# A five-block transformer stack on one core: the last feed-forward block works on one tile of tokens behind the other, and three row maxima of the attention passes stand in other units

## The chip, the core and the metric

The program runs on one core of one Trainium2 chip. The core has five engines with a queue of instructions each: TensorE (PE, matmuls; PEld is its weight load), VectorE (DVE), ScalarE (ACT), GpSimd (POOL) and SyncE (SP), which here issues every DMA. They meet only at semaphores. The metric is the device time of one execution in microseconds (us), lower is better.

## The reference, cut to what matters

One sequence of 256 tokens with 512 features, and a context of 4096 rows of 128 features, pass six residual blocks. The change touches the fourth in part, the fifth's last steps and the whole of the sixth:

```python
x = x + _L0_xattn_ref(_layernorm(x), ctx_512, ...)
x = x + _L0_attn_ref(_layernorm(x), ...)
x = x + _L0_ffn_ref(_layernorm(x), ...)      # 32 experts
x = x + _L1_xattn_ref(_layernorm(x), ctx_512, ...)   # 16 heads over 4096 keys
x = x + _L1_attn_ref(_layernorm(x), ...)     # gated state space; its output is y * rsqrt(mean(y*y)+eps) @ W_out
x = x + _L1_ffn_ref(_layernorm(x), w_gate_up, w_down)

def _quant_dequant(v, axis):                 # 8 bits, one scale for each row
    scale = jnp.max(jnp.abs(v), axis=axis, keepdims=True) / 127.0
    scale = jnp.maximum(scale, 1e-8)
    return jnp.clip(jnp.round(v / scale), -127, 127) * scale
def _L1_ffn_ref(x, w_gate_up, w_down):       # 512 -> 2 * 1408 -> 512
    gate_up = quant(x) @ quant(w_gate_up).T
    gate, up = split(gate_up)
    h = silu(gate) * up
    return quant(h) @ quant(w_down).T
```

The scale of a token's inner row `h` needs the maximum over all 1408 inner values before any of them can be rounded.

## The kernel before, in words

Each engine's program is written out by hand, block after block; nothing is scheduled by a planner. A wait on a semaphore holds up all that stands behind it on its engine.

**The fourth block** (attention over 4096 keys) runs in `XP = 8` passes over pairs of heads, each of `NCH = 8` units `c` of 512 keys, each unit of four quarters `e`. In a quarter PE turns a tile of probabilities (`turn`), ACT takes it out of PSUM (`pH`, line 856), DVE takes the low part (`pL`, line 1198), and PE weighs the values with both (`weigh`). Beside that, pass `p` makes the scores of pass `p + 1`, which DVE copies out with their maxima (`scores_out`, line 1145): four tiles in each of the units 1 to 7 (those of the unit ahead), none in unit 0, and in unit 7 the four of the last unit as well, followed by the row maxima `nmX` without which ACT cannot start the exponentials. Units 3 to 6 also add a finished output to `x` on DVE (`add_out`, line 1157).

In the same passes the weights of the sixth block are quantized in the background: 15 jobs (`JOBS`), three in a pass, so passes 0 to 4. `row_max` on DVE takes the maximum of 128 rows in two halves (line 1164, in quarters 1 and 3 of the unit), and the scale and its inverse (lines 1170, 1172); SP stores them and loads the next rows (`rows`); POOL rounds a tile of the weights (`round_columns`) and SP stores it (`columns`). `ROWS_AT` names the three units: 1, 4 and 7. The halves are of 704 elements in the first four jobs (pass 0 and the first job of pass 1) and of 512 in the others.

**The fifth block's end.** For eight tiles `m` DVE makes `yz`, ACT `yn` and its square `y2`; POOL sums the squares, and PE multiplies `yn` with `wout` (`project`, line 1753). PE sums the squares over partitions (lines 1778, 1779), DVE and POOL make the root `yrs`, and DVE adds the projected rows, times `yrs`, to `x` (line 1296).

**The sixth block** has two tiles `t` of 128 tokens. LayerNorm of both, one `row_scales` over both (lines 1221 to 1223), rounding in fp32 by adding and subtracting a constant (`xr` on DVE, `xq` on ACT), eight transposes on PE, one copy `xqT` on ACT. Then eight chunks `n`, four for each token tile, of 352 gate and 352 up columns: eight matmuls (line 1799), `gs` and `us` on DVE, Silu on ACT (`sgF`), the product `hF` on POOL. After a token tile's four chunks: the maximum over 1408 elements on DVE (`hs`), rounding (`hr`, `hq`), eleven transposes (line 1806), the copy `hqT` on ACT, eleven matmuls with `w_down` (line 1812), `of` and `x` on DVE. `swb` holds the weights' scales, broadcast to all partitions. One DMA stores `out`. `stay_awake(count, bank)` (line 1339) issues `count` matmuls of 512 columns on constants whose result nobody reads; they stand where PE would wait.

Of the kernel before, what the change touches and what calls it, by code (L numbers as in the profile page):

```python
# [92 lines left out]
def perceiver(nc, a, out):  # L93
    ctx = ExitStack()
    with ctx:
# [578 lines left out]
        def _(act):  # L674
# [273 lines left out]
            act.wait_ge(late_pe.sem, late_pe.at("xqT", 1))
            act.activation(xqT[:], PSb[:, 0, :].rearrange("p (k t) -> p k t", t=T), ACT.Copy).then_inc(late_act.sem, 1)

            def integers(t):
                act.wait_ge(hr_ready, t + 1)
                act.activation(hq[:, t], hr[:, t], ACT.Copy, bias=-ROUND).then_inc(hq_ready, 1)
# [8 lines left out]
            for t in range(NT):  # L962
                if t:
                    integers(t)
                act.wait_ge(late_pe.sem, late_pe.at("hqT", t + 1))
# [935 lines left out]
```

## Time and profile before

| | |
|---|---|
| median of 3 runs | 1056.04 us (1053.2 to 1057.41) |
| profiled execution, its own time | 1053.18 us |
| its span | 1051.5 us |
| busy: PE, DVE, ACT, POOL | 94%, 70%, 55%, 28% of the span |
| chain that ended last | PE 76%, DVE 14%, ACT 5%, issue 2% |
| fourth block's passes | 440 to 935 us of the span |
| fifth block | 936 to 1013 us |
| sixth block | 1013 to 1051.5 us |

Busy times are shares of the span; the chain of waits is followed back from the last instruction, and only what lies on it can shorten the kernel. The program's own time is 1.7 us above the span.

### The profile page before, as it was taken

How to read it: one execution, taken by the hardware profiler on the slowest of the kernel's cores; microseconds unless marked ns; L12 is line 12 of the kernel's file. 1: busy time of each engine (PE TensorE's matmuls, PEld its weight loads, DVE VectorE, ACT ScalarE, POOL GpSimd, SP SyncE). 2: the span in 40 equal slices, each digit the busy share in tenths (PEclk: the TensorE clock that was granted, in tenths of full speed). 3: DMA queues.
4: the chain of work that ended last, by engine and by line, in shares of the span. 5: the costliest groups of instructions: out<-in, count | busy, mean ns of one | idle time of the engine just before them, and what ended most of it. 6: DMA issues, size and time to landing. Idle time of an engine off the chain costs nothing.

```text
span 1051.5 us, 18010 instructions
## 1 busy us (share of the span) xinstructions
PE 990.6 (94%) x6641; PEld 788.4 (75%) x6641; DVE 732.6 (70%) x1434; ACT 575.1 (55%) x1251; POOL 291.2 (28%) x210
## 2 busy tenths in 40 slices
PE   7989989999998799999998999989899999989996
PEld 5545689999997576687787777878788787968653
DVE  3566456555553789788787888878877787658555
ACT  3445344444443320486776667767676777837633
POOL 6910144444442300000000422313225504013412
PEclk9999999999999999999999999999999999999999
DMA  8560076656632233201113347423323203083010
GB/s 269 130 242 1 4 231 245 213 210 209 209 121 82 83 95 101 71 29 28 52 46 54 61 92 103 91 53 77 76 58 95 72 1 96 8 295 162 1 66 21
DMA packets 65966, 109.18 MB, mean 104 GB/s; under 512 B 19393, under 2 KB 44129, under 8 KB 64738
## 3 DMA queue, kind: packets, MB, share of 16 engines
q1 hardware_dynamic: 65890, 108.17, 35.3%
q8 instruction: 47, 0.77, 0.3%
q14 instruction: 29, 0.24, 0.1%
HBM read 103.24 MB, written 4.91 MB: 103 GB/s over the span
## 4 chain that ended last, share of the span: by engine, by line
PE 76%; DVE 14%; ACT 5%; issue 2%; DMA 1%; POOL 1%; SPq 0%; DVEq 0%; ACTq 0%; POOLq 0%
PE PS L1618 14%; PE PS L1491 12%; PE PS L1607 9%; PE PS L1595 8%; PE PS L1510 5%; DVE scores L1145 3%; PE PS L1580 3%; PE PS L1710 3%; PE PS L1632 2%; PE PS L1339 2%; DVE pL L1198 2%; PE PS L1753 1%; ACT scores L832 1%; PE PS L1391 1%; PE PS L1550 1%
## 5 line engine op out<-in xcount | busy, mean ns | idle before, releaser
L1198 DVE TENSOR_TENSOR pL<-PS,pH 128x512 fp32r<-128x512 f32 x256 | 175.9, 687 | 66.0 <-ACT pH L856 65.5
L856 ACT ACTIVATE pH<-PS 128x512 fp32r<-128x512 f32 x256 | 151.7, 595 | 99.9 <-PE PS L1607 99.9
L832 ACT ACTIVATE scores<-scores,nmX 128x512 f32<-128x512 f32 x256 | 185.2, 723 | 26.3 <-DVE nmX L1149 26.3
L1145 DVE TENSOR_SCALAR_CACHE_REDUCE scores<-PS 128x512 f32<-128x512 f32 x256 | 172.6, 682 | 18.8 <-PE PS L1595 18.4
L1618 PE MATMUL PS<-pH,kvH 128*128 128x256 f32 x512 | 164.4, 321 | 7.4 <-ACT xnT L841 7.4
L1607 PE MATMUL PS<-ident,scores 128*128 128x128 f32 x1024 | 157.3, 276 | 4.5 <-DVE pL L1198 4.3
L1607 PEld LDWEIGHTS PS<-ident,scores 128*128 128x128 f32 x1024 | 117.0, 140 | 36.6 <-issue 16.4
L1618 PE MATMUL PS<-pL,kvH 128*128 128x256 f32 x512 | 143.9, 281 | 0.0
L1618 PE MATMUL PS<-pH,kvL 128*128 128x256 f32 x512 | 143.7, 281 | 0.0
L1618 PEld LDWEIGHTS PS<-pH,kvH 128*128 128x128 f32 x512 | 96.7, 189 | 11.6 <-issue 11.4
L614 POOL TENSOR_TENSOR xn<-xn,winvB 128x1024 f32<-128x1024 f32 (+1 forms) x17 | 39.6, 2330 | 211.0 <-DMA xn<-in_w1t 114.3
L1618 PEld LDWEIGHTS PS<-pL,kvH 128*128 128x128 f32 x512 | 97.2, 190 | 0.0
L1618 PEld LDWEIGHTS PS<-pH,kvL 128*128 128x128 f32 x512 | 96.4, 188 | 0.0
L1052 DVE TENSOR_TENSOR gL<-rawG,gH 128x1536 fp32r<-128x1536 f32 x16 | 56.9, 3554 | 29.4 <-ACT gH L715 29.3
L578 POOL TENSOR_TENSOR dL<-rawD,dH 128x1536 fp32r<-128x1536 f32 x16 | 56.4, 3526 | 47.1 <-ACT dH L759 47.1
L1595 PE MATMUL PS<-keyH,qsH 64*128 64x512 f32 x256 | 58.4, 453 | 8.6 <-DVE scores L1145 8.2
L1491 PE MATMUL PS<-xH,gH 128*128 128x256 f32 x192 | 54.7, 285 | 3.2 <-DVE uL L1052 2.9
L599 POOL TENSOR_TENSOR wkrL<-wkr,wkrH 128x128 fp32r<-128x128 f32 x8 | 4.2, 524 | 191.0 <-ACT wkrH L796 191.0
L1595 PEld LDWEIGHTS PS<-keyH,qsH 64*128 64x128 f32 x256 | 24.0, 183 | 42.9 <-issue 24.5
L1491 PE MATMUL PS<-xH,uH 128*128 128x256 f32 x192 | 54.9, 286 | 0.0
L1491 PE MATMUL PS<-xL,uH 128*128 128x256 f32 x192 | 54.9, 286 | 0.0
L1491 PE MATMUL PS<-xH,uL 128*128 128x256 f32 x192 | 54.9, 286 | 0.0
(305 smaller groups left out, 2250.1 us busy)
## 6 DMA issues: line engine op xcount, KB each, us to landing
rawG<-in_wg SPq DMA_DIRECT2D x16, 768.0 KB, 5.7
rawU<-in_wu SPq DMA_DIRECT2D x16, 768.0 KB, 7.2
rawD<-in_wd SPq DMA_DIRECT2D x16, 768.0 KB, 6.4
wrow<-in_w SPq DMA_DIRECT2D x11, 512.0 KB, 5.5
xn<-in_w1t SPq DMA_DIRECT2D x11, 512.0 KB
wturned<-turned SPq DMA_DIRECT2D x4, 1056.0 KB, 13.5
wb<-w_rows SPq DMA_DIRECT2D x32, 128.0 KB, 3.3
wqX<-in_wqX SPq DMA_DIRECT2D x16, 256.0 KB, 2.6
```

Of the source, the lines that this page charges most:

```text
L578: pool.tensor_tensor(dL[:, b].rearrange("p m n -> p (m n)"), rawD[:, b], dH[:, b].rearrange("p m n -> p (m n)").bitcast(F32), ALU.subtract ...
L614: step(pool.tensor_tensor(part.rearrange("p (k o) -> p k o", o=shape[2]), part.rearrange("p (k o) -> p k o", o=shape[2]), inverse, ALU.mult))
L832: act.activation(at, at, ACT.Exp, bias=nmX[:, p % 2, h, q:q + 1], accum_out=csum[:, p % 2, NT * h + q, c:c + 1]).then_inc(exp_done, 1)
L856: act.activation(pH[:, i % 4], PS[:, 2 + i % 2, :].rearrange("p (k t) -> p k t", t=T), ACT.Copy).then_inc(pH_ready, 1)
L1052: dve.tensor_tensor(lo[b][:].rearrange("p k m n -> p (k m n)"), raw[:, b], hi[b][:].rearrange("p k m n -> p (k m n)").bitcast(F32), ALU.su ...
L1145: dve.tensor_scalar(sp_[:, h, q, c * CH:(c + 1) * CH], PS[:, 4 * q + h, :], 1.0, None, ALU.mult, ALU.max, accum_out=cmax[:, h, q, c:c + 1] ...
L1198: dve.tensor_tensor(pL[:, i % 4], PS[:, 2 + i % 2, :].rearrange("p (k t) -> p k t", t=T), pH[:, i % 4].bitcast(F32), ALU.subtract).then_in ...
L1491: mm = pe.matmul(PS[:, 3 * b + m, j * T:(j + 1) * T], w[b][:, kt, m, :], v[:, kt, :], start=(kt == 0 and c == 0), stop=(kt == KT - 1 and c ...
L1510: mm = pe.matmul(PS[:, 6 + t, :], h[:, b, m, t * P:(t + 1) * P], w[:, b, m, :], start=(first and m == 0 and c == 0), stop=(last and m == 2 ...
L1595: mm = pe.matmul(PS[:, 4 * q + h, :], w[rank, p % 2, q * P:(q + 1) * P], v[rank, c * CH:(c + 1) * CH], start=(j == 0), stop=(j == 2), skip ...
L1607: mm = pe.transpose(PS[:, 2 + i % 2, m * T + q * P:m * T + (q + 1) * P], sp_[:, h, q, tile * P:(tile + 1) * P], ident[:])
L1618: mm = pe.matmul(PS[:, 6, h * T:(h + 1) * T], w[:, 4 * c + 2 * u + m, :], v[:, i % 4, m, :], start=(i == 0 and m == 0 and k == 0), stop=(c ...
```

## The change

`ROWS_AT` becomes 1, 3, 5. In the sixth block the two token tiles run one behind the other: tile 0's input is normalized, rounded, turned and copied alone, and tile 1's follows in ACT's and PE's queues behind the first two chunks. The maximum over 1408 is taken in four of 352 (`chunk_max`), each two chunks late, and then over those four. Rounding, transposes, copies and the second product are cut into parts (`PARTS`): two for tile 0, three for tile 1, one of whose copies is DVE's. `stay_awake` goes from 6 to 0 ahead of the last projection, from 40 to 24 and from 4 to 3 about the input's transposes, from 8 to 0 ahead of tile 0's inner transposes, and from 8 to 10 ahead of tile 1's. The sums of squares move ahead of the last projection. `swb` is laid over the dead weights `win` and loaded as soon as these are read; the output is stored tile by tile.

```diff
-ROWS_AT = (1, 4, 7)
+PARTS = (((0, 8, 6), (8, FT, 7)), ((0, 4, 4), (4, 8, 5), (8, FT, 2)))
+ROWS_AT = (1, 3, 5)
...
-        swb = A("swb", [P, (GT + DT) * P])
+        swb = win[:].rearrange("p k n -> p (k n)")[:, 0:(GT + DT) * P]
+        hmx = A("hmx", [P, NT, 4])
...
-            sp.wait_ge(x_done, 5)
-            sp.dma_start(swb[:], s_rows[:].partition_broadcast(P)).then_inc(swb_in, 16)
-            sp.wait_ge(x_done, 6)
-            sp.dma_start(out.rearrange("o (t p) d -> p (o t) d", p=P), x[:]).then_inc(stored, 16)
-            sp.wait_ge(stored, 16)
+            sp.wait_ge(ssm_pe.sem, ssm_pe.at("z3", 1))
+            sp.dma_start(swb, s_rows[:].partition_broadcast(P)).then_inc(ffn_in, 16)
+            for t in range(NT):
+                sp.wait_ge(x_done, 6 + t)
+                sp.dma_start(out.rearrange("o (t p) d -> p (o t) d", p=P)[:, t], x[:, t]).then_inc(stored, 16)
+            sp.wait_ge(stored, 16 * NT)
...
+            input_integers(0)
             for n in range(4 * NT):
                 act.wait_ge(gs_ready, n + 1)
                 if n >= 2:
                     act.wait_ge(hF_ready, n - 1)
                 act.activation(sgF[:, n % 2], gs[:, n % 2], ACT.Silu, scale=sx[:, n // 4:n // 4 + 1]).then_inc(late_act.sem, 1)
+                if n == 1:
+                    input_integers(1)
                 if n == 6:
-                    integers(0)
...
+                    integers(0, 0)
+                    integers(0, 1)
+            turned_part(0, 0)
+            turned_part(0, 1)
+            integers(1, 0)
+            integers(1, 1)
+            turned_part(1, 0)
+            integers(1, 2)
+            turned_part(1, 2)
...
+            gated_out(0)
+            ln_stats(0)
+            gated_out(1)
             dve.sem_inc(x_done, 1)
...
+            input_rounded(0)
+            ln_stats(1)
+            input_rounded(1)
+            dve.wait_ge(ffn_in, 80)
+
+            def chunk_max(n):
+                t, c = n // 4, n % 4
+                dve.wait_ge(hF_ready, n + 1)
+                dve.tensor_reduce(hmx[:, t, c:c + 1], hF[:, t, c * FC:(c + 1) * FC], AX.X, ALU.max, apply_absolute_value=True).then_inc(dve_step, 1)
+                step.n += 1
 
             def rounded(t):
-                dve.wait_ge(hF_ready, 4 * (t + 1))
-                row_scales(hs[:, t:t + 1], hsi[:, t:t + 1], hF[:, t])
-                dve.tensor_scalar(hr[:, t], hF[:, t], hsi[:, t:t + 1], ROUND, ALU.mult, ALU.add).then_inc(hr_ready, 1)
+                dve.wait_ge(dve_step, step.base + step.n)
+                row_scales(hs[:, t:t + 1], hsi[:, t:t + 1], hmx[:, t])
+                for a_, b_, bank in PARTS[t]:
+                    dve.tensor_scalar(hr[:, t, a_ * P:b_ * P], hF[:, t, a_ * P:b_ * P], hsi[:, t:t + 1], ROUND, ALU.mult, ALU.add).then_inc(hr_ready, 1)
...
+                if n >= 2:
+                    chunk_max(n - 2)
                 if n == 5:
                     rounded(0)
+            chunk_max(4 * NT - 2)
+            chunk_max(4 * NT - 1)
             rounded(1)
+            a_, b_, bank = PARTS[1][1]
+            dve.wait_ge(late_pe.sem, late_pe.at("hqT1", 2))
+            dve.tensor_copy(hqT[:, a_:b_, P:T], PSb[:, bank, 0:(b_ - a_) * P].rearrange("p (k t) -> p k t", t=P)).then_inc(hqT_mid, 1)
...
+            stay_awake(24, 4)
+            pe.wait_ge(late_dve.sem, late_dve.at("ms", 1))
+            turn_input(0)
+            stay_awake(3, 4)
+            pe.wait_ge(late_act.sem, late_act.at("xqT0", 1))
+            pe.wait_ge(ffn_in, 80)
             for n in range(4 * NT):
                 t, c = n // 4, n % 4
                 if n >= 2:
                     pe.wait_ge(us_ready, n - 1)
+                if n == 2:
+                    turn_input(1)
+                if n == 4:
+                    pe.wait_ge(late_act.sem, late_act.at("xqT1", 1))
...
+            turn_part(0, 0)
+            turn_part(0, 1)
+            pe.wait_ge(hqT_ready, 1)
+            down_part(0, 0)
+            pe.wait_ge(hqT_ready, 2)
+            down_part(0, 1)
             pe.wait_ge(us_ready, 4 * NT)
-            stay_awake(8, 2)
-            turn_inner(1)
-            down_inner(1)
+            stay_awake(10, 2)
+            turn_part(1, 0)
+            turn_part(1, 1)
...
```

**DVE in pass 4, unit 7.** `pL` is the low part of the probabilities, `scores,cmax` a tile of the next pass's scores with its maximum, `nmX` the row maximum, `wmax`, `wscale`, `winv` the weight rows' job. Before:

```order
L1164 TENSOR_REDUCE wmax<-wrow 128x1 [waits wrow_in]
L1145 TENSOR_SCALAR scores,cmax<-PS 128x512 [waits sX_ps]
L1139 TENSOR_TENSOR keyL<-PS,keyH 128x512 [waits keyH_ready]
L1198 TENSOR_TENSOR pL<-PS,pH 128x512 [waits pH_ready]
L1145 TENSOR_SCALAR scores,cmax<-PS 128x512 [waits sX_ps] x2
L1149 TENSOR_REDUCE nmX<-cmax 128x1 [waits sX_out]
L1145 TENSOR_SCALAR scores,cmax<-PS 128x512 [waits sX_ps]
L1149 TENSOR_REDUCE nmX<-cmax 128x1 [waits sX_out]
L1198 TENSOR_TENSOR pL<-PS,pH 128x512 [waits pH_ready]
L1164 TENSOR_REDUCE wmax<-wrow 128x1
L1170 TENSOR_SCALAR wscale<-wmax 128x2 [waits scale_stored,dve_step]
L1172 RECIPROCAL winv<-wscale 128x2 [waits wscale_ready]
```

Now, the same stretch:

```order
L1158 TENSOR_TENSOR keyL<-PS,keyH 128x512 [waits keyH_ready]
L1217 TENSOR_TENSOR pL<-PS,pH 128x512 [waits pH_ready]
L1164 TENSOR_SCALAR scores,cmax<-PS 128x512 [waits sX_ps] x2
L1168 TENSOR_REDUCE nmX<-cmax 128x1 [waits sX_out]
L1164 TENSOR_SCALAR scores,cmax<-PS 128x512 [waits sX_ps]
L1168 TENSOR_REDUCE nmX<-cmax 128x1 [waits sX_out]
L1217 TENSOR_TENSOR pL<-PS,pH 128x512 [waits pH_ready]
L1164 TENSOR_SCALAR scores,cmax<-PS 128x512 [waits sX_ps]
L1168 TENSOR_REDUCE nmX<-cmax 128x1 [waits sX_out]
```

The two reductions and the two small operations behind them are gone from here.

**DVE in pass 4, unit 5**, the unit to which they move (now; `x<-PS,recX,x` is the addition of a finished output):

```order
L1183 TENSOR_REDUCE wmax<-wrow 128x1 [waits wrow_in]
L1164 TENSOR_SCALAR scores,cmax<-PS 128x512 [waits sX_ps]
L1158 TENSOR_TENSOR keyL<-PS,keyH 128x512 [waits keyH_ready]
L1217 TENSOR_TENSOR pL<-PS,pH 128x512 [waits pH_ready]
L1164 TENSOR_SCALAR scores,cmax<-PS 128x512 [waits sX_ps]
L1217 TENSOR_TENSOR pL<-PS,pH 128x512 [waits pH_ready]
L1183 TENSOR_REDUCE wmax<-wrow 128x1
L1189 TENSOR_SCALAR wscale<-wmax 128x2 [waits scale_stored,dve_step]
L1191 RECIPROCAL winv<-wscale 128x2 [waits wscale_ready]
```

They stand between the same neighbours as they do in unit 4 of before.

**PE at the end of the fifth block and the start of the sixth.** `busyB` rows are those of `stay_awake`, `ones` rows the sums of squares, `wout,yn` the last projection, `identb,xq` the input's transposes. Before:

```order
L1753 MATMUL PS<-wout,yn 128x512 [waits yn_ready]
L1753 MATMUL PS<-wout,yn 128x512
L1339 MATMUL PS<-busyB,identE 128x512 x6
L1753 MATMUL PS<-wout,yn 128x512 [waits yn_ready]
L1778 MATMUL PS<-ones,y2s 128x1 [waits decay_ready,y2_ready,y2_added]
L1779 MATMUL PS<-ones,y 128x1
L1778 MATMUL PS<-ones,y2s 128x1
L1779 MATMUL PS<-ones,y 128x1
L1753 MATMUL PS<-wout,yn 128x512
L1339 MATMUL PS<-busyB,identE 128x512 x40
```

Now:

```order
L1793 MATMUL PS<-wout,yn 128x512 [waits yn_ready]
L1793 MATMUL PS<-wout,yn 128x512
L1815 MATMUL PS<-ones,y2s 128x1 [waits decay_ready,y2_ready,y2_added]
L1816 MATMUL PS<-ones,y 128x1
L1815 MATMUL PS<-ones,y2s 128x1
L1816 MATMUL PS<-ones,y 128x1
L1793 MATMUL PS<-wout,yn 128x512 [waits yn_ready]
L1793 MATMUL PS<-wout,yn 128x512
L1379 MATMUL PS<-busyB,identE 128x512 x24
L1826 MATMUL PS<-identb,xq 128x128 [waits late_act,late_dve]
L1826 MATMUL PS<-identb,xq 128x128 x3
L1379 MATMUL PS<-busyB,identE 128x512 x3
```

The sums of squares now stand ahead of both projections, and the first token tile is turned alone; the second tile's four transposes stand behind sixteen matmuls of the first two chunks.

## Rows read from the trace of the kernel before

**Rows 1.** The page: span and instructions.

```profile
span 1051.5 us, 18010 instructions
```

**Rows 2.** Timeline, ACT: `pH` opening unit 7 and the next pass; start, length.

```profile
490.08 0.60 ACT L856 ACTIVATE pH<-PS 128x512 fp32r<-128x512 f32 x1 [1.49 <-PE PS L1607]
501.31 0.58 ACT L856 ACTIVATE pH<-PS 128x512 fp32r<-128x512 f32 x1
...
748.71 0.60 ACT L856 ACTIVATE pH<-PS 128x512 fp32r<-128x512 f32 x1 [1.49 <-PE PS L1607]
759.35 0.58 ACT L856 ACTIVATE pH<-PS 128x512 fp32r<-128x512 f32 x1
...
813.21 0.60 ACT L856 ACTIVATE pH<-PS 128x512 fp32r<-128x512 f32 x1 [1.49 <-PE PS L1607]
822.40 0.58 ACT L856 ACTIVATE pH<-PS 128x512 fp32r<-128x512 f32 x1
```

**Rows 3.** Chain that ended last, pass 4 unit 7: start, length, what.

```profile
751.24 0.59 DVE wmax L1164
```

**Rows 4.** Windows: units 4, 4, 5, 6 of passes 4, 5, 4, 4; busy by engine.

```profile
726.00:733.90 7.90, 7.90 (x60) 6.42 (x59) 7.30 (x19) 5.47 (x14) 3.94 (x3) 1.00 0.01 2
790.50:798.40 7.90, 7.90 (x60) 6.42 (x59) 6.38 (x15) 5.47 (x14) 3.94 (x3) 1.00 0.31 60
733.90:741.80 7.90, 7.90 (x59) 6.42 (x59) 6.78 (x15) 5.47 (x14) 0.00 (x0) 1.00 0.81 137
...
741.80:748.80 7.00, 7.00 (x57) 6.15 (x57) 5.70 (x13) 5.44 (x14) 3.19 (x2) 1.00 0.55 147
```

**Rows 5.** Timeline, all engines, end of fifth block and input of sixth.

```profile
1007.06 0.40 ACT L938 ACTIVATE y<-yz 128x256 f32<-128x256 f32 x1
...
1010.38 0.16 DVE L1291 TENSOR_SCALAR ss<-PS 128x2 f32<-128x2 f32 x1 [3.78 <-PE PS L1779]
...
1011.15 8.80 PE L1339 MATMUL PS<-busyB,identE 128*128 128x512 bf16 x40
...
1011.43 1.54 DVE L1296 SCALAR_TENSOR_TENSOR x<-PS,yrs,x 128x512 f32<-128x512 f32 x2 [0.88 <-POOL yrs L666]
...
1018.34 0.88 DVE L1304 TENSOR_SCALAR xr<-xn,sxi 128x512 f32<-128x512 f32 x2
1018.86 1.15 ACT L947 ACTIVATE xq<-xr 128x512 bf16<-128x512 f32 x2 [11.41 <-DVE xr L1304]
```

**Rows 6.** Timeline, the eight chunks and the second product.

```profile
1021.58 10.07 PE L1799 MATMUL PS<-wturned,xqT 128*128 128x352 bf16 x64 [0.25 <-ACT xqT L949]
1023.06 0.53 DVE L1322 TENSOR_TENSOR gs<-PS,swb 128x352 f32<-128x352 f32 x1 [3.83 <-PE PS L1799]
...
1030.14 1.61 DVE L1221 TENSOR_REDUCE hs<-hF 128x1 f32<-128x1408 f32 x1
...
1035.51 0.79 PE L1806 MATMUL PS<-identb,hq 128*128 128x128 bf16 x11 [2.13 <-ACT hq L953]
1036.07 0.92 POOL L671 TENSOR_TENSOR hF<-sgF,us 128x352 f32<-128x352 f32 x1 [0.82 <-ACT sgF L959]
...
1044.05 2.55 PE L1812 MATMUL PS<-wturned,hqT 128*128 128x512 bf16 x11 [1.44 <-ACT hqT L966]
1046.71 0.69 DVE L1330 TENSOR_TENSOR of<-PS,swb 128x512 f32<-128x512 f32 x1 [4.92 <-PE PS L1812]
...
1048.27 0.39 SPq L502 DMA_DIRECT2D out<-x  x1
```

**Rows 7.** The tile wmax: lengths in ns, min/median/max.

```profile
L1164 DVE TENSOR_REDUCE wmax<-wrow x30: 674/677/877, 449.7 to 756.7; 128x1 f32<-128x512 f32 x22, 128x1 f32<-128x704 f32 x8
```

**Rows 8.** Timeline, PE, in the third block, and the window after (PEclk third from last).

```profile
146.32 0.39 PE L1491 MATMUL PS<-xH,gH 128*128 128x256 f32 x1 [2.88 <-DVE uL L1052]
...
147.70:151.10 3.40, 3.40 (x18) 3.40 (x17) 0.96 (x1) 2.03 (x2) 1.33 (x1) 0.50 0.28 100
```

**Rows 9.** DMA issues: KB each, median us to landing.

```profile
out<-x SPq DMA_DIRECT2D x1, 512.0 KB, 2.8
```

More of the change, by code:

```diff
@@ L942, in _, with input_integers, integers, turned_part @@
                     weighted_late(UA + 1)
-            for t in range(NT):
+            def input_integers(t):
                 act.wait_ge(late_dve.sem, late_dve.at("xr", t + 1))
                 act.activation(xq[:, t], xr[:, t], ACT.Copy, bias=-ROUND).then_inc(late_act.sem, 1)
[L948 to L953, printed above, removed]
+                act.wait_ge(late_pe.sem, late_pe.at(f"xqT{t}", 1))
+                act.activation(xqT[:, :, t * P:(t + 1) * P], PSb[:, 6 + t, 0:D].rearrange("p (k t) -> p k t", t=P), ACT.Copy).then_inc(late_act.sem, 1)
+            def integers(t, part):
+                a_, b_, bank = PARTS[t][part]
+                act.wait_ge(hr_ready, t * len(PARTS[0]) + part + 1)
+                act.activation(hq[:, t, a_ * P:b_ * P], hr[:, t, a_ * P:b_ * P], ACT.Copy, bias=-ROUND).then_inc(hq_ready, 1)
+            def turned_part(t, part):
+                a_, b_, bank = PARTS[t][part]
+                act.wait_ge(late_pe.sem, late_pe.at(f"hqT{t}", part + 1))
+                act.activation(hqT[:, a_:b_, t * P:(t + 1) * P], PSb[:, bank, 0:(b_ - a_) * P].rearrange("p (k t) -> p k t", t=P), ACT.Copy).then_inc(hqT_ready, 1)
+            input_integers(0)
             for n in range(4 * NT):
@@ L1317, in _ @@
                 t, c = n // 4, n % 4
-                dve.wait_ge(late_pe.sem, late_pe.at("guF", n + 1))
+                dve.wait_ge(late_pe.sem, late_pe.at(*gate(n)))
                 if n >= 2:
-                    dve.wait_ge(late_act.sem, late_act.at("sgF", n - 1))
+                    dve.wait_ge(late_act.sem, late_act.at(*activated(n - 2)))
                     dve.wait_ge(hF_ready, n - 1)
@@ L1801, in _, with turn_part, down_part @@
                 mm.then_inc(late_pe.sem, 1)
-            def turn_inner(t):
-                pe.wait_ge(hq_ready, t + 1)
-                for m in range(FT):
-                    mm = pe.transpose(PSb[:, 6 - 2 * t + m // 8, (m % 8) * P:(m % 8 + 1) * P], hq[:, t, m * P:(m + 1) * P], identb[:])
+            def turn_part(t, part):
+                a_, b_, bank = PARTS[t][part]
+                pe.wait_ge(hq_ready, t * len(PARTS[0]) + part + 1)
+                for m in range(a_, b_):
+                    mm = pe.transpose(PSb[:, bank, (m - a_) * P:(m - a_ + 1) * P], hq[:, t, m * P:(m + 1) * P], identb[:])
                 mm.then_inc(late_pe.sem, 1)
-            def down_inner(t):
-                pe.wait_ge(hqT_ready, t + 1)
-                for m in range(FT):
+            def down_part(t, part):
+                a_, b_, bank = PARTS[t][part]
+                for m in range(a_, b_):
                     mm = pe.matmul(PS[:, t, :], hqT[:, m, t * P:(t + 1) * P], w2T[:, m, :], start=(m == 0), stop=(m == FT - 1))
-                mm.then_inc(inner_done, 1)
-            stay_awake(8, 1)
-            turn_inner(0)
-            down_inner(0)
-            pe.wait_ge(us_ready, 4 * NT)
-            stay_awake(8, 2)
-            turn_inner(1)
-            down_inner(1)
+                if b_ == FT:
+                    mm.then_inc(inner_done, 1)
+            turn_part(0, 0)
[4 more added lines that the diff above has]
+            down_part(0, 1)
+            pe.wait_ge(us_ready, 4 * NT)
+            stay_awake(10, 2)
+            turn_part(1, 0)
+            turn_part(1, 1)
+            pe.wait_ge(hqT_ready, 3)
+            down_part(1, 0)
+            turn_part(1, 2)
+            pe.wait_ge(hqT_mid, 1)
+            down_part(1, 1)
+            pe.wait_ge(hqT_ready, 4)
+            down_part(1, 2)
 def rope_table(length, dim):
```

57 lines of the change are left out of this document (24 added, 33 removed).

## The prediction

> **What bounds the kernel now.** I read the page first (the span, [rows 1]), then the chain that ended last, then the timeline where it leaves PE. Over the whole span PE carries three quarters of the chain, so an edit on another engine counts only where PE waits for it. There are two such places. The first is unit 7 of each attention pass: between the `pH` that opens it and the one that opens the next pass lie 10.64 us in pass 4, which has a row maximum there, and 9.19 us in pass 5, which has none; in pass 0 it is 11.23 us, with the longer halves [rows 2]. The chain runs over DVE here, through the reduction itself [rows 3]. In unit 4, where a row maximum also stands, DVE's busy time rises from 6.38 us (pass 5) to 7.30 us (pass 4), yet PE is busy for 7.90 us of 7.90 in both [rows 4]: the same work costs nothing there. The second place is the sixth block, a string of steps that each wait for the one before. From the first addition to `x` at 1011.43 to the first gate matmul at 1021.58 pass 10.15 us [rows 5, 6]; the eight chunks last from 1023.06 to the end of the last `hF` at 36.99 us past 1000, 13.93 us; then come 11.3 us to the store's issue and 3.2 us to the end [rows 6].
>
> **The row maxima.** What leaves unit 7 is worth 10.64 - 9.19 = 1.45 us in pass 4. Passes 1 to 3 have the same work there, so four passes give 5.8 us; pass 0 gives 11.23 - 9.19 = 2.04 us. That is 7.8 us if units 3 and 5 take the work for nothing. Do they? Unit 5 of pass 4 carries what spills over from unit 4: 6.78 us against unit 4's 6.38 without the work, so one job and its spill fill 7.30 + 6.78 = 14.08 us of 15.80. Moved to unit 3, the job spills into unit 4 instead, which is as long. Moved from 7 to 5, it makes unit 5 about 7.30 and unit 6 about 5.70 + 0.40 = 6.10 us, of 7.90 and 7.00: 13.4 of 14.9 us [rows 4]. So there are some 1.5 us of idle DVE left before unit 7 begins, and no debt should reach it. In pass 0 there is no addition to `x`, units are shorter and the halves longer (877 ns against 677, [rows 7]), so I give back 0.6 us there. I take **-7.2 us**; bounds -7.8 (nothing lost) and 0.4 of it, about -3, if every job in units 3 and 5 costs what half a unit-7 job does.
>
> SP's and POOL's queues move with it. SP loads the next rows behind each job; jobs now lie two units (15.8 us) apart and four over the pass's seam, and a load takes a few us, so DVE's wait for rows stays hidden. POOL's rounding of the columns waits for loads that SP issues earlier, and nothing on the chain waits for it until after the last pass.
>
> **The fifth block's end.** `y` is complete at 1007.46, but the sums stood behind six constant matmuls and a projection, and `ss` began at 1010.38. Now the four small matmuls start at about 1007.5 and take the 0.8 us that lie between those of before, so `ss` comes at 1008.45: **-1.9 us**, if the first projection (1 us on PE) is done when `yrs` is, which it is by 0.1 us [rows 5].
>
> **The input.** From the first addition, for tile 0: addition 0.77, statistics 1.05, tile 1's addition 0.77 (with POOL's root beside it), LayerNorm's application 0.58, maximum over 512 elements 0.70 (677 ns, [rows 7]), two scalings 0.40, `xr` 0.44: 4.7 us, then `xq` 0.65 [rows 5], so 5.4 us. PE has meanwhile 0.85 us of projection left and 24 constant matmuls, each 8.80 / 40 = 0.22 us: 6.05 us, so these are the later by 0.6. Then transposes 0.3, copy of half a tile 0.6, handover 0.1: 7.05 against 10.15 us, **-3.1 us**. The scales' load is behind DVE's wait for PE today and is issued earlier now; it costs nothing.
>
> **The chunks.** Three things add, two take away.
> - PE turns tile 1 behind chunk 1. `xq` of tile 1 stands on ACT behind the second Silu; PE ends chunk 1 some 2.0 us before it can turn, so chunk 2 is +2.0 us late.
> - A chunk costs DVE 0.44 + 0.48 us; with its maximum over 352 elements (0.5 us, on the line through 512: 677 and 1408: 1614 ns, [rows 6, 7]) it is 1.45 us, above PE's 10.07 / 8 = 1.26. Six chunks of it: some +1.2 us.
> - The one reduction of 1.61 us behind chunk 5 becomes 0.2: -1.4; rounding in two parts +0.1.
> - ACT rounds 1024 and 384 elements (1.5 us) ahead of the last Silu, and the earlier end of the reductions no longer hides it: +0.5.
>
> Together **+2.3 us**, so the last `hF` ends 16.2 us after the first `gs`, and 2.5 us earlier than now.
>
> **The second product.** After the last `hF`: its maximum 0.5, 0.6 for the scales, `hr` of 512 elements 0.44, `hq` 0.6. It does not decide: tile 0's second product starts when ACT has copied its transposes (1.0 us after the last Silu), takes 2.55 us [rows 6], and behind it stand ten constant matmuls, 2.2 us. PE comes to tile 1's transposes 4.9 us after the last `hF`, some 2.5 us after `hq` is there. From there: transposes 0.5, copy 0.5, first part 0.9, transposes 0.2, the rest 1.8, `of` and `x` 1.45. `x` is complete 10.1 us after the last `hF` against 11.2 today: **-1.1 us**. DVE's own copy has no row; I take 0.55 us (between `xq`'s 0.57 and nothing), and twice that would cost 0.5. The store of 512 KB lands 2.8 us after its issue [rows 9]; half of it can save between nothing and 1 us, I take **-0.3**.
>
> Sum of the sixth block with the fifth's end: -1.9 - 3.1 + 2.3 - 1.1 - 0.3 = -4.1 us, at full clock.
>
> **The clock.** In the third block PE was idle for 2.88 us up to 146.32, and from 147.7 to 151.1 its granted clock was 0.50, which is 1.2 of 2.4 GHz; an idle time of 2.13 us before the inner transposes left it at full speed [rows 6, 8]. The change makes PE idle for about 2.0 us behind chunk 1, and takes away the eight constant matmuls ahead of tile 0's inner transposes: there I count 3.0 us of waiting, 0.5 of transposes and 1.5 of waiting again. So the second gap is long enough for the fall, the first is at the border. A stretch of 3.4 us at half clock under tile 0's product and the ten constant matmuls costs up to 1.7 us, and nothing if it ends first. I take **+1.3 us**; bounds 0 and +3.4 (both gaps).
> [...]
>
> Total: -7.2 - 4.1 + 1.3 = **-10.0 us**.
>
> **The rivals.**
> - *The tail gives nothing* (0.16). Both gaps drop the clock, and a gate chunk takes 2.4 us instead of 1.26 for three chunks, 1.5 us beyond DVE's pace; with the 1.7 above, DVE's copy at 1.1 us and the extra maxima fully exposed the 4.1 us shrink to nothing. For it: PE's gaps. Against it: 4.1 us is more than each alone. Result -7.2 us.
> - *DVE runs full in units 3 to 6* (0.14). Row maxima in 3 and 5 push a debt through unit 6 into unit 7. For it: unit 3 also has ACT's work for the next keys and both units an addition to `x`. Against it: [rows 4], unit 4 has that addition too. Half of 7.2 is lost: -6.4 us.
> - *The 1.45 us are not the reduction's* (0.06). Pass 5 might be quick because other work is gone from it. Against it: the chain [rows 3]. Result -2.8 us, within what is no change.
> - *Slower* (0.04). A job in unit 3 or 5 stalls PE for its full 1.7 us on DVE: two jobs in each of five passes cost 17 us, 7.8 come back from unit 7, 2.8 from the tail: +6 us. It takes over from the point where a job costs PE more than (7.8 + 2.8) / 10 = 1.1 us; in unit 4 it costs 0.0 today.
> - The forecast (0.60).
>
> **How the numbers follow.** The sum is made against the profiled execution's own 1053.18 us: 1043.2. That execution lies at the low end of the runs shown, whose median is 1056.04 (2.9 higher); by that the result is 1046.0. The mean of all four readings is 1055.0, and I predict **1045.0 us**. The bounds of the unknown terms (-7.8 to -3, clock 0 to 3.4, copy and store +-0.5) and the spread of the runs give 1040.5 to 1049.5; it takes in most of the first two rivals. A measurement of this kernel can tell 0.5%, 5.3 us, from no change. Faster by more: the forecast, and three quarters of the first two rivals with a rest for runs that spread, 0.85; within: 0.11; slower: 0.04.
>
> **What would show it.** Passes 0 to 4 last as long as pass 5 (unit 7 at 9.2 us) and units 3 and 5 stay at 7.9. `ss` begins 1.0 us after the last `y`; the first gate matmul 7 us after the first addition to `x`; gate chunks 1.45 us apart from chunk 2 on; PE waits about 2 us before tile 1's input transposes; ten constant matmuls end after `hq` is ready; a PEclk of 0.5 appears between tile 0's inner transposes and tile 1's. Wrong I would be if a unit 3, 5 or 6 grew by more than 0.3 us, or if the half clock fell on the gate matmuls.

## The result and the profile after

The changed kernel takes 1046.65 us (median of 5 runs, 1046.3 to 1047.16), the kernel before 1056.04: a ratio of 0.9899 (95% interval 0.9867 to 0.9932). Timed again it took 1047.39 beside 1057.04 (0.9918, 0.9877 to 0.9959). The page of its profiled execution, 1046.65 us; PEclk is the granted clock in tenths, in 40 slices:

```profile
span 1044.7 us, 17977 instructions
...
PE 990.0 (95%) x6612; PEld 789.3 (76%) x6612; DVE 734.7 (70%) x1449; ACT 575.3 (55%) x1257; POOL 290.8 (28%) x210
...
PEclk9999999999999899999999999999999999999998
```

**The passes.** The timeline of ACT, after: the `pH` that opens pass 0, unit 7 of pass 0 and pass 1, then unit 7 of pass 4 and pass 5.

```profile
443.22 0.59 ACT L864 ACTIVATE pH<-PS 128x512 fp32r<-128x512 f32 x1
...
493.25 0.60 ACT L864 ACTIVATE pH<-PS 128x512 fp32r<-128x512 f32 x1 [1.49 <-PE PS L1647]
...
502.45 0.57 ACT L864 ACTIVATE pH<-PS 128x512 fp32r<-128x512 f32 x1
...
746.18 0.60 ACT L864 ACTIVATE pH<-PS 128x512 fp32r<-128x512 f32 x1 [1.49 <-PE PS L1647]
...
755.36 0.58 ACT L864 ACTIVATE pH<-PS 128x512 fp32r<-128x512 f32 x1
```

and the first of these in the trace of before, whose pass 5 opens at 759.35 [rows 2]:

```profile
440.38 0.58 ACT L856 ACTIVATE pH<-PS 128x512 fp32r<-128x512 f32 x1
```

Unit 7 is 9.20 us in pass 0 and 9.18 in pass 4 (11.23 and 10.64 before). Passes 0 to 4 together fall from 318.97 to 312.14 us, by 6.83. In pass 0, of the units 1 to 6 those with a row job last 7.38 us and those without it 7.03, before and after, so there the moved job is not free. The first pass opens 2.84 us later than before, in code that the change does not touch: 0.25 us of it are there by 290 us, and 2.6 come where two stretches of half clock fell, which the profiled execution of before did not have (windows of after: us; busy time and instructions of PE, PEld, DVE, ACT, POOL; granted clock, DMA share, GB/s):

```profile
338.80:342.20 3.40, 3.06 (x15) 2.47 (x13) 3.19 (x6) 2.43 (x5) 0.00 (x0) 0.51 0.92 314
359.30:362.70 3.40, 3.40 (x10) 2.67 (x9) 2.09 (x6) 0.60 (x1) 0.00 (x0) 0.50 0.18 58
```

**The sixth block.** The timeline of after, from the last `y` of the fifth block to the store:

```profile
1003.00 0.40 ACT L946 ACTIVATE y<-yz 128x256 f32<-128x256 f32 x1
...
1004.56 0.16 DVE L1310 TENSOR_SCALAR ss<-PS 128x2 f32<-128x2 f32 x1 [2.01 <-PE PS L1816]
...
1005.61 0.75 DVE L1316 SCALAR_TENSOR_TENSOR x<-PS,yrs,x 128x512 f32<-128x512 f32 x1 [0.88 <-POOL yrs L674]
...
1012.44 2.56 PE L1845 MATMUL PS<-wturned,xqT 128*128 128x352 bf16 x16
...
1014.22 0.52 DVE L1355 TENSOR_TENSOR gs<-PS,win 128x352 f32<-128x352 f32 x1
...
1016.94 0.38 PE L1826 MATMUL PS<-identb,xq 128*128 128x128 bf16 x4 [1.94 <-ACT xq L955]
...
1019.92 0.52 DVE L1355 TENSOR_TENSOR gs<-PS,win 128x352 f32<-128x352 f32 x1
...
1020.84 0.51 DVE L1336 TENSOR_REDUCE hmx<-hF 128x1 f32<-128x352 f32 x1
...
1021.27 0.51 DVE L1355 TENSOR_TENSOR gs<-PS,win 128x352 f32<-128x352 f32 x1
...
1027.80 0.89 PE L1853 MATMUL PS<-identb,hq 128*128 128x128 bf16 x11 [2.75 <-ACT hq L962]
...
1028.78 0.93 POOL L679 TENSOR_TENSOR hF<-sgF,us 128x352 f32<-128x352 f32 x1 [0.91 <-ACT sgF L974]
1029.60 4.87 PE L1859 MATMUL PS<-wturned,hqT 128*128 128x512 bf16 x11 [0.91 <-ACT hqT L967]
...
1031.39 1.15 ACT L962 ACTIVATE hq<-hr 128x512 bf16<-128x512 f32 x2 [1.47 <-DVE hr L1343]
1034.26 2.77 PE L1379 MATMUL PS<-busyB,identE 128*128 128x512 bf16 x10
1036.87 0.61 PE L1853 MATMUL PS<-identb,hq 128*128 128x128 bf16 x8
...
1037.52 0.42 DVE L1367 COPY hqT<-PS 128x512 bf16<-128x512 bf16 x1 [5.44 <-PE PS L1853]
...
1041.43 0.75 DVE L1371 SCALAR_TENSOR_TENSOR x<-of,hs,x 128x512 f32<-128x512 f32 x1
```

The first gate matmul comes 6.83 us behind the first addition to `x` (10.15 before); PE stands 1.94 us ahead of tile 1's input transposes; the chunks are 1.35 us apart; and tile 0's second product takes 4.87 us where it took 2.55 [rows 6]. The windows of after say why: half clock, and full clock ahead of it.

```profile
1028.30:1035.10 6.80, 5.89 (x19) 2.06 (x17) 2.77 (x9) 2.77 (x5) 0.93 (x1) 0.50 0.00 0
...
1012.40:1028.30 15.90, 11.17 (x78) 6.51 (x78) 13.21 (x32) 8.02 (x13) 6.50 (x7) 1.00 0.00 1
```

From the last `y` to the end of the span: 1051.5 - 1007.06 = 44.4 us before, 1044.7 - 1003.00 = 41.7 after. So the spans differ by 6.8 us = 6.83 (passes 0 to 4) + 2.7 (tail) + 0.1 (between) - 2.84 (ahead of pass 0). The two stages that the change touches give 9.5 us, the medians 9.4.

### The profile page after: what moved, and what is told of

It is laid out like the page before. It is cut to its first block, busy times and chain, and to the rows that moved or that the text cites. A ratio compares the mean times of both kernels' runs of the same rounds, so it can differ in the third digit from the quotient of the medians.

```text
span 1044.7 us, 17977 instructions
## 1 busy us (share of the span) xinstructions
PE 990.0 (95%) x6612; PEld 789.3 (76%) x6612; DVE 734.7 (70%) x1449; ACT 575.3 (55%) x1257; POOL 290.8 (28%) x210
## 4 chain that ended last, share of the span: by engine, by line
PE 77%; DVE 13%; ACT 5%; issue 2%; DMA 1%; POOL 1%; SPq 0%; DVEq 0%; POOLq 0%; ACTq 0%
PE PS L1658 16%; PE PS L1531 12%; PE PS L1647 10%; PE PS L1635 8%; PE PS L1550 6%; PE PS L1620 4%; PE PS L1750 3%; DVE scores L1164 2%; PE PS L1672 2%; ACT scores L840 1%; PE PS L1431 1%; PE PS L1793 1%; PE PS L1590 1%; PE PS L1379 1%; PE PS L1599 1%
```

## The experiments

The runs of one kernel scatter by half a per cent and more to either side (before: 1050.83 to 1062.75 over 22 runs), so beside each median stand two stretches of its profiled execution, read as above, and the half clock between the last `y` and the last addition.

| kernel | median (us) | ratio, interval | passes 0-4 | last y to end | half clock, tail |
|---|---|---|---|---|---|
| before | 1056.04 | | 318.97 | 44.4 | none |
| after | 1046.65 | 0.9899 (0.9867-0.9932) | 312.14 | 41.7 | 6.8 |
| e1_rows_only | 1053.37 | 0.9961 (0.9926-0.9997) | 312.7 | 46.1 | 3.4 |
| e2_tail_only | 1053.07 | 0.9959 (0.9926-0.9992) | 319.0 | 42.2 | 2 x 3.4 |
| e3_warm8 | 1047.78 | 0.9904 (0.9874-0.9934) | 312.2 | 42.2 | 2 x 3.4 |
| e4_no_ten | 1043.5 | 0.9884 (0.9833-0.9935) | 312.9 | 39.2 | 6.8 |
| e5_xq_early | 1044.53 (1 run) | | 312.2 | 41.4 | 6.8 |
| e6_whole_max | 1049.0 (1 run) | | 313.8 | 42.6 | 2 x 3.4 |
| e7_rows024 | 1048.13 (1 run) | | 312.8 | 42.2 | 2 x 3.4 |
| e8_warm_lean | 1043.04 | 0.9862 (0.9793-0.9932) | 314.4 | 36.7 | none |
| e9_after_again | 1047.39 | 0.9918 (0.9877-0.9959) | 312.9 | 41.9 | 6.8 |
| e10_lean_again | 1041.24 | 0.9873 (0.9840-0.9906) | 314.5 | 36.5 | none |
| e11_scale_apart | 1043.44 | 0.9871 (0.9832-0.9911) | 311.5 | 42.6 | 3.4 + 6.8 |
| e12_lean_scale_apart | 1040.11 | 0.9849 (0.9808-0.9889) | 311.5 | 36.5 | none |

**e1_rows_only**: before, with the new places of the row maxima. **e2_tail_only**: after, with the old ones.

```diff
-ROWS_AT = (1, 4, 7)
+ROWS_AT = (1, 3, 5)
```

> The kernel before with nothing changed but the units of the row maxima, 1, 3 and 5 instead of 1, 4 and 7. Theory (the reduction in unit 7 delays the maxima and with them the exponentials, in unit 5 it is hidden, in unit 3 nearly): passes 0 to 4 are shorter by 1.2 to 1.7 us each, 6.8 us in all, unit 7 at 9.2 us, unit 4 at 8.1 in passes 2 to 4; the stretch from the last y to the end stays at 44.4 us. Time 0.65% below the kernel before. Rival (the gain in the passes comes from something else that the change did, such as the memory that the scales no longer take): passes as before, same time.

> The changed kernel with the row maxima back in units 1, 4 and 7. Theory (the two parts add): passes as in the kernel before, 10.6 us for unit 7; from the last y to the end 41.7 us instead of 44.4; time 0.25% below the kernel before. Rival (the feed-forward part gives nothing on average, the profiled execution was a lucky one): no less than 44 us for that stretch.

The passes follow the table of places alone, the tail follows the rest. The medians would not have told this: they fell by 0.39% and 0.41% where 0.65% and 0.25% were expected, each with 0.35% to either side. Passes 0 to 4 of e1 are shorter by 6.2 us, not 6.8; a unit 6 of 7.48 us in pass 2 takes most of the rest. The tail of e1 should have been that of before and is 1.7 us longer, because the half clock fell there, behind the same idle times of 2.13 and 1.44 us that had left it full in the profiled execution of before [rows 6]. The timeline of PE in e1_rows_only:

```profile
1027.40 0.79 PE L1806 MATMUL PS<-identb,hq 128*128 128x128 bf16 x11 [2.13 <-ACT hq L953]
1029.62 4.23 PE L1812 MATMUL PS<-wturned,hqT 128*128 128x512 bf16 x11 [1.44 <-ACT hqT L966]
```

**e3_warm8** puts the eight constant matmuls back; **e4_no_ten** takes away the ten.

```diff
+            stay_awake(8, 1)
             turn_part(0, 0)
```

```diff
             pe.wait_ge(us_ready, 4 * NT)
-            stay_awake(10, 2)
             turn_part(1, 0)
```

> The changed kernel with the eight constant matmuls back ahead of tile 0's inner transposes. Theory (the half clock under tile 0's second product comes from PE's wait before these transposes): granted clock 1.0 there, the eleven matmuls take 2.55 us instead of 4.87, the ten constant ones 2.2, and the last y to the end is 38.7 to 39.5 us instead of 41.7. Rival (PE's later wait for ACT's copy, 0.9 us, and the thin transposes are enough to lower the clock): the clock falls all the same, 41 us or more.

> The changed kernel without the ten constant matmuls ahead of tile 1's inner transposes. Theory (hq is ready some 4 us before PE comes to it, so these matmuls only delay): 2.5 us less from the last y to the end, 39.2 us. Rival (they keep the clock up for what follows, and without them tile 1's second product runs at half clock): of the 2.8 us that go, 1.5 to 2.5 come back, 41 us.

The theory of e3 missed and its rival held: PE's wait before the transposes fell from 2.75 to 1.03 us, but the clock fell all the same, one gap earlier, behind PE's wait for `xq` of tile 1, and again under the second product. The second fall came behind two waits of only 1.03 and 1.01 us. Timeline of PE and windows of e3_warm8:

```profile
1016.98 0.38 PE L1826 MATMUL PS<-identb,xq 128*128 128x128 bf16 x4 [1.95 <-ACT xq L955]
...
1031.16 4.23 PE L1859 MATMUL PS<-wturned,hqT 128*128 128x512 bf16 x11 [1.01 <-ACT hqT L967]
```

```profile
1017.50:1020.90 3.40, 3.40 (x14) 1.77 (x12) 1.44 (x3) 1.08 (x2) 0.17 (x1) 0.51 0.00 0
1031.20:1034.60 3.40, 3.40 (x9) 1.19 (x10) 2.20 (x7) 1.43 (x3) 0.06 (x1) 0.50 0.00 0
```

The theory of e4 held. The first two parts of tile 1's `hq` are ready at 1032.5 in after, but PE reaches its transposes at 1036.87, behind the ten: without them the tail is 2.5 us shorter, though the half clock is still there.

**e5_xq_early**: ACT rounds tile 1's input ahead of the first Silu; its second part keeps its place.

```diff
             input_rounded_off(0)
             input_turned(0)
+            input_rounded_off(1)
...
                 if n == 1:
-                    input_integers(1)
+                    input_turned(1)
```

> The changed kernel with tile 1's xq on ACT ahead of the first Silu instead of behind the second; its copy xqT stays behind the second. Theory (PE's wait of 1.9 us before tile 1's input transposes is ACT's order): the wait falls to under 0.3 us, gs of chunk 2 comes 2.7 us behind gs of chunk 0 instead of 4.3, and all later gs are earlier by 1.6 us or more. The end gains less while PE is late for tile 1's inner transposes: the last y to the end at 40 us if the clock falls as before. Rival (DVE's pace of 1.35 us per chunk takes it back): gs of chunk 5 earlier by under 0.5 us.

PE's wait fell from 1.94 to 0.29 us, yet the sixth `gs` comes 7.92 us behind the first, against 8.40 (1022.62 - 1014.22), and the end gains 0.3: under 0.5, as the rival said, but not for its reason. The wait moved: the Silu's table load now stands behind the rounding, so the first Silu begins 2.06 us after the first `gs` (0.55 in after); the third `gs` has to wait for the first `hF`, and PE waits 1.09 us for the third `us`. Timeline of e5_xq_early:

```profile
1012.67 0.63 ACT L955 ACTIVATE xq<-xr 128x512 bf16<-128x512 f32 x1 [1.96 <-DVE xr L1326]
1013.32 1.28 ACT L978 ACT_TABLE_LOAD   x1
...
1013.62 0.40 PE L1830 MATMUL PS<-identb,xq 128*128 128x128 bf16 x4 [0.29 <-DVE us L1360]
...
1015.59 0.57 ACT L959 ACTIVATE xqT<-PS 128x512 bf16<-128x512 bf16 x1
```

**e6_whole_max**: one reduction over all of `hF` in the place of the chunks' maxima.

```diff
-                row_scales(hs[:, t:t + 1], hsi[:, t:t + 1], hmx[:, t])
+                row_scales(hs[:, t:t + 1], hsi[:, t:t + 1], hF[:, t])
...
-                if n >= 2:
-                    chunk_max(n - 2)
...
-            chunk_max(4 * NT - 2)
-            chunk_max(4 * NT - 1)
```

> The changed kernel with the maximum over all 1408 elements in one reduction again, the rest as changed. Theory (the chunk maxima cost 0.13 us of pace per chunk and save the long reduction twice): chunks 1.24 us apart, gs of chunk 6 later by 1.0 us, hr of tile 1 complete 2 us later behind the last hF; the end the same or later by under 0.7 us, since PE comes late to tile 1's transposes anyway. Rival (the chunk maxima only cost): the last hF earlier and the end earlier by 1 us.

At full clock its chunks are 1.20 and 1.28 us apart, against 1.35, and the reduction of 1.61 us comes back behind them; the tail is 0.9 us longer, clock included. The half clock lies elsewhere than in after, though; in e2 and e7, whose tail is that of after, it lies in the same two places as here, and beside these the tail is 0.4 us longer. The maxima by chunks are worth about that. Timeline of DVE in e6_whole_max:

```profile
1023.17 0.52 DVE L1355 TENSOR_TENSOR gs<-PS,win 128x352 f32<-128x352 f32 x1 [1.09 <-PE PS L1841]
1024.37 0.53 DVE L1355 TENSOR_TENSOR gs<-PS,win 128x352 f32<-128x352 f32 x1 [0.18 <-PE PS L1841]
1025.65 0.53 DVE L1355 TENSOR_TENSOR gs<-PS,win 128x352 f32<-128x352 f32 x1 [0.27 <-PE PS L1841]
1026.58 1.61 DVE L1240 TENSOR_REDUCE hs<-hF 128x1 f32<-128x1408 f32 x1
```

**e7_rows024**: row maxima in units 0, 2 and 4, where no scaling should meet POOL's work.

```diff
-ROWS_AT = (1, 3, 5)
+ROWS_AT = (0, 2, 4)
```

> The changed kernel with the row maxima in units 0, 2 and 4. Theory (the 0.24 us that unit 4 of passes 2 to 4 still loses come from DVE's small scaling at the end of unit 3, which waits until the GpSimd instruction that began just before it has ended, 1.37 us instead of 0.17): no scaling longer than 0.17 us falls on a unit with PE busy throughout unless a GpSimd instruction runs beside it, and where one does, the scaling ends when that one ends, within 0.05 us; passes 1 to 4 at 63.05 us, if none does in units 0, 2, 4. Pass 0 loses up to 2.5 us once, for the first rows have not landed. Rival (the lost 0.24 us are DVE's load in units 3 and 4 as such): a unit 2 or 4 with a row maximum loses 0.2 us with no long scaling.

All scalings were short (0.17 us), and unit 4 fell to 7.88 us, but unit 2 rose from 7.89 to 8.19 in passes 1 to 4, with POOL idle: the sign that the rival had named. Passes 1 to 4 take 63.35 to 63.37 us, not 63.05. The trace has the wait: half a row maximum now stands ahead of `keyL`, which ends 4.80 us after the unit's opening `pH` instead of 4.20, and PE waits for it before it multiplies a finished head with `woX` (line 1716 of after), for both use the same PSUM bank. In unit 4, which also has a row job, `keyL` ends at 4.33 us, and PE does not wait. Timeline of e7_rows024, whose unit 2 of pass 2 opens at 581.81, then of after, where it opens at 580.84:

```profile
585.92 0.69 DVE L1158 TENSOR_TENSOR keyL<-PS,keyH 128x512 fp32r<-128x512 f32 x1
586.66 0.30 PEld L1672 LDWEIGHTS PS<-woX,xnT 128*128 128x128 f32 x2 [0.25 <-DVE keyL L1158]
```

```profile
584.36 0.68 DVE L1158 TENSOR_TENSOR keyL<-PS,keyH 128x512 fp32r<-128x512 f32 x1
```

**e8_warm_lean** and, beside an unchanged control, **e10_lean_again**: e5's edit, no ten constant matmuls, eight ahead of tile 0's inner transposes and three behind.

```diff
+            stay_awake(8, 1)
             turn_part(0, 0)
             turn_part(0, 1)
+            stay_awake(3, 1)
             pe.wait_ge(hqT_ready, 1)
...
-            stay_awake(10, 2)
```

> The changed kernel with three edits: tile 1's xq ahead of the first Silu, no constant matmuls ahead of tile 1's inner transposes, and eight ahead of tile 0's and three behind them. Theory (PE's waits, not DVE's work, set what is left, and the clock falls for lack of work): no half clock from the gates to the end in most executions, eleven matmuls in 2.55 us, the last y to the end 36.0 to 36.8 us instead of 41.7, time 1.5% below the kernel before. Rival (the clock falls all the same): 38 us.

> The changed kernel once more, unchanged, as the control for the version with the lean tail on the same chip. The stages of its tail should stand as before: from the last y to the end of the span between 40 and 43 us, with the half clock somewhere between the gate chunks and the second product. Both theories (the lean tail is truly shorter; the lean tail was only lucky with the clock) expect the same of this run: a median of 1044 to 1050 us.

> The lean tail once more (tile 1's rounding ahead of the first Silu, eight constant matmuls before and three after tile 0's inner transposes, none before tile 1's), timed on the same chip as the unchanged one. Theory: its tail is shorter by 5 us because no half clock falls from the gates on and PE has ten constant matmuls less before tile 1; last y to end 36 to 37.5 us, and the median 3 to 6 us under that of the changed kernel in this call. Rival: the place at which the clock falls is chance, and the first look was a lucky one; then the half clock comes back between the gates and the second product, last y to end is 39 to 42 us, and the medians differ by less than 2 us.

Timed beside each other: 1041.24 us (1039.41 to 1044.26) against 1047.39 (1045.63 to 1052.54) for the unchanged one, e9, whose tail and half clock came out as in after; no run of the one is as slow as any of the other. The tail is 36.7 and 36.5 us long, without a half clock. No run separates which of the three edits keeps the clock. Window and timeline of e10_lean_again:

```profile
1004.00:1033.60 29.60, 26.31 (x153) 13.01 (x154) 23.24 (x56) 13.40 (x22) 8.49 (x10) 1.00 0.01 2
```

```profile
1025.52 0.79 PE L1857 MATMUL PS<-identb,hq 128*128 128x128 bf16 x11 [1.03 <-ACT hq L964]
...
1027.32 2.55 PE L1863 MATMUL PS<-wturned,hqT 128*128 128x512 bf16 x11 [0.36 <-ACT hqT L969]
```

But its passes 0 to 4 are 2.4 us longer than after's: unit 6 of pass 2 lasts 8.49 us there, not 7.03. The timeline of e10_lean_again at the end of unit 5 shows DVE's scaling of 0.17 us taking 2.29, until POOL's multiplication ends:

```profile
607.18 2.38 POOL L622 TENSOR_TENSOR xn<-xn,winvB 128x1024 f32<-128x1024 f32 x1 [10.59 <-DMA xn<-in_w2t]
607.30 2.29 DVE L1193 TENSOR_SCALAR wscale<-wmax 128x2 f32<-128x2 f32 x1
...
608.42 0.60 ACT L864 ACTIVATE pH<-PS 128x512 fp32r<-128x512 f32 x1 [2.35 <-PE PS L1651]
...
616.91 0.60 ACT L864 ACTIVATE pH<-PS 128x512 fp32r<-128x512 f32 x1 [1.83 <-PE PS L1651]
```

The long scalings of all traces, read together, give the price. The one at the end of unit 5 sets the length of the unit 6 behind it, which is 7.02 us with a short one:

| trace, pass | scaling (us) | unit 6 (us) |
|---|---|---|
| e3 pass 3 | 0.74 | 7.04 |
| e1 pass 2 | 1.28 | 7.48 |
| e4 pass 4 | 1.52 | 7.71 |
| e9 pass 4 | 1.57 | 7.76 |
| e8 pass 4 | 1.59 | 7.81 |
| e10 pass 4 | 1.71 | 7.91 |
| e8 pass 2 | 2.14 | 8.36 |
| e10 pass 2 | 2.29 | 8.49 |
| e6 pass 2 | 2.33 | 8.53 |

Up to about 0.8 us it costs next to nothing; beyond that every microsecond costs one. At the end of unit 3, 1.37 us cost 0.24. In before a scaling of 1.41 us stood at the end of unit 1 of pass 3, and unit 2 kept its 7.89: there no addition to `x` follows at once. Where one does (units 3 to 6), PE waits for it before the next keys (`oX_added`, line 1710 of after), for the two share a PSUM bank.

**e11_scale_apart** and **e12_lean_scale_apart** scale one column at a time, the first in after, the second in the lean version.

```diff
-                    dve.tensor_scalar(wscale[:], wmax[:], 1.0 / QMAX, QEPS, ALU.mult, ALU.max).then_inc(wscale_ready, 1)
+                    count = 1 if n < DT else 2
+                    for c in range(count):
+                        ins = dve.tensor_scalar(wscale[:, c:c + 1], wmax[:, c:c + 1], 1.0 / QMAX, QEPS, ALU.mult, ALU.max)
+                        if c < count - 1:
+                            step(ins)
+                    ins.then_inc(wscale_ready, 1)
...
-                    dve.reciprocal(winv[:], wscale[:]).then_inc(winv_ready, 1)
+                    dve.reciprocal(winv[:, 0:count], wscale[:, 0:count]).then_inc(winv_ready, 1)
```

> The changed kernel, with the scaling of a row job, one 128x2 instruction before, as instructions of 128x1 (one for the second matrix's rows, two for the first's). In the traces so far a 128x2 scaling that meets a POOL TENSOR_TENSOR ends with it (0.17 us becomes 1.37, and up to 2.33), and the unit behind it is longer: unit 4 by 0.24 us in passes 2 to 4, unit 6 of pass 2 or 4 by 0.7 to 1.5 us in some executions; a 128x1 scaling of the tail (hs) ran its 0.15 us in the middle of a POOL TENSOR_TENSOR. Theory (the two instructions exclude each other, and the wait stretches the units): no scaling over 0.2 us, unit 4 at 7.88 in all passes, unit 6 at 7.03, passes 0 to 4 together 311.5 us (312.1 to 312.9 now), median 0.5 to 1.5 us lower than the 1046.65 to 1047.4 of the unchanged one. Rival 1 (a scaling waits for POOL for some other reason): the long scalings stay. Rival 2 (the long scaling is a bystander, and the load of DVE and ACT in the unit is what counts): scalings at 0.17, unit 4 still at 8.12, passes as now.

> The lean tail with the same edit of the scaling. Theory: passes 0 to 4 take 311.5 us where the two looks at the lean tail had 314.4 and 314.5 (a unit 6 of 8.5 us in pass 2 and of 7.9 in pass 4 in both), last y to end stays at 36.5 to 37 us, so the median falls by 1.5 to 3 us under the lean tail's 1041.24 and 1043.04: 1038.5 to 1041. Rivals as in the run before: then passes 0 to 4 stay at 313 to 314.5 and the median at 1041 to 1043.

The theory held to a tenth of a microsecond, and both rivals fell: no long scaling, unit 4 at 7.88 in passes 1 to 4 of both and unit 6 at 7.03 us in all, passes 0 to 4 at 311.5. The job's places are those of after, so in e11 the load of DVE in units 3 and 5 alone costs nothing from pass 1 on. The tile `wscale` in e11_scale_apart, then in e10_lean_again (ns, min/median/max):

```profile
L1191 DVE TENSOR_SCALAR wscale<-wmax x26: 153/153/156, 457.7 to 737.9; 128x1 f32<-128x1 f32 x26
```

```profile
L1193 DVE TENSOR_SCALAR wscale<-wmax x15: 169/170/2285, 453.2 to 735.3; 128x2 f32<-128x2 f32 x15
```

e11's median, 1043.44 us, is 3 to 4 us under that of after, more than the 0.5 to 1.5 expected and than the 0.6 that its profiled execution shows in the passes; executions that would have had a long unit 6 may save more, but with a scatter of 8 us in its own runs I don't settle the size by medians. e12 has the lowest median, 1040.11 us (1036.34 to 1042.89) beside 1055.78 for before; by medians alone it can't be told from e10.

## Why the prediction was right, step by step

The 1045.0 us and the range held, and so did the mechanism of both parts: the reductions leave the unit whose exponentials wait for DVE, and the sixth block's steps overlap. The sum was -10.0 us against -9.5 in the two stages. That the parts add up so well is luck: in the tail the clock cost 1.7 us more than taken, and the second product, the store, the chunks and the input were better by 0.6, 0.5, 0.4 and 0.2. The base was loose too: the mean of "all four readings" counts the profiled execution twice, once as 1053.2 us among the three runs; those alone average 1055.6.

- **Row maxima** (-7.2, measured -6.83). That unit 7 falls to 9.2 us held: 2.03 + 4 x 1.45 = 7.8 us left it, and no debt reached it. Pass 0 gave back 0.33 (0.6 taken); its units 3 and 5 grew from 7.03 to 7.38 us, one of them in exchange for unit 4. From pass 1 on "units 3 and 5 stay at 7.9" held. Missed was unit 4, 8.12 us in passes 2 to 4 of after, up to 0.24 more each, and a unit 6 of 7.5 to 8.5 us in a pass or two of e1, e4, e6 and e8 to e10. Pass 0's units and these are above the 0.3 us that I had named as the sign of being wrong. The step that failed is the count of DVE's idle time: it took the scaling at its usual 0.17 us, and it asked for DVE's share of a unit where PE waits for single results of DVE. e11 and e12 show the cause and its price, 0.6 us in after and 3.0 in e10.
- **Fifth block's end** (-1.9, measured -1.8): last `y` to `ss` 3.32 us before, 1.56 after.
- **Input** (-3.1, measured -3.3). PE's side adds up to 0.85 + 24 x 0.22 = 6.13 us, not the 6.05 that I wrote.
- **Chunks** (+2.3, measured +1.9 from the first gate matmul to the last `hF`: 17.27 us against 15.41). The terms as listed add up to +2.4, and with the two items above the last `hF` would come 2.7 us earlier, not 2.5. PE's wait of 2.0 us was there with 1.94, the pace 1.35 instead of 1.45: DVE's next instruction begins 0.1 us before the one ahead of it ends (1020.84 + 0.51 against 1021.27). I had taken `gs` and `us` from start to start and the maximum with its full length.
- **Second product** (-1.1) and **clock** (+1.3): together +0.2, measured +1.3 (last `hF` to the last `x` complete: 12.47 us against 11.2). The clock was mis-sized. Under the half clock the eleven matmuls cost 2.3 us more, the ten constant ones about 0.6, the transposes 0.1: +3.0, and -1.7 at full clock. I had priced a stretch of 3.4 us; it lasted 6.8. My steps of the second product add up to 10.25 us behind the last `hF`, not 10.1; and in the first rival such a stretch holds one and a half chunks of 2.4 us, not three.
- **Store** (-0.3, measured -0.8: last `x` to the end 3.3 us before, 2.5 after). **DVE's copy** 0.42 us (0.55 taken).

The rival that the tail gives nothing fell, though its condition came: in five of nine traces of the new tail (e2, e3, e6, e7, e11) the half clock lay under the gate matmuls as well, which I had named as a sign of being wrong, and the tail still gained 1.8 to 2.2 us. The rival that DVE runs full was right in direction and wrong in cause and size: unit 7 stayed at 9.2 us everywhere. That the half clock is bound to a gap "long enough for the fall" was my model, and it fails: by e1 and before, idle times of 2.13 and 1.44 us drop it in one execution and not in another, and in e3 it fell behind 1.03 and 1.01 us. Only the tail whose longest wait is 1.1 us kept it at 1.00 each time, in three traces of three; the nine of the new tail with longer waits all have a fall, though not in the same gap. This agrees in direction with the Trainium skill, "TensorE: Matmul & The Clock Gate", Part 1, by which the array runs at half clock by default and activity releases the throttle; what decides in which gap it falls, no run here shows.

Open stays that, and why two stretches of half clock ahead of pass 0 come in some executions only.

## What to carry to other kernels

Read the gain of a moved instruction from the unit that it leaves, and its price from what runs on the *other* engines where it lands, since a tiny instruction can wait for a long one of POOL; and ask which single result of the engine PE waits for next, not only how busy the engine is. Where executions scatter by as much as an edit is worth, compare stages of traces and add up the medians last. Constant matmuls belong where PE waits anyway; behind a product that nothing delays they are only work in the way (2.5 us here).

## What the runs showed of the hardware

Eleven traces have scalings of 128x2 that took more than 0.2 us, 50 in all, and each of the 50 ended within 0.03 us of the end of a POOL TENSOR_TENSOR that was running when it began; POOL's instruction kept its length. Two that began 0.08 and 0.05 us ahead of POOL's (e1, e6) kept their 0.17 us. Timeline of after, DVE and POOL:

```profile
594.45 2.39 POOL L622 TENSOR_TENSOR xn<-xn,winvB 128x1024 f32<-128x1024 f32 x1
594.78 0.67 DVE L1183 TENSOR_REDUCE wmax<-wrow 128x1 f32<-128x512 f32 x1
595.49 1.37 DVE L1189 TENSOR_SCALAR wscale<-wmax 128x2 f32<-128x2 f32 x1
```

The reduction beside the same POOL instruction kept its 0.67 us, and scalings of 128x1 kept 0.15 (all 52 of e11 and e12, 21 of them beside a POOL TENSOR_TENSOR). So the engines do not meet only at semaphores. This agrees with the Trainium skill, "SBUF — State Buffer", section "🔬 SBUF: two separate sides": a DVE instruction that uses both of its port pairs and a GpSimd instruction exclude each other for the whole length of the one that came first. That two elements are enough for it, and one is not, is what these runs add.
